# A feed-forward branch spread over 46 instead of 41 gaps, and half of an elementwise product moved from VectorE to GpSimd

## The reference, cut to what matters

```python
h = concat([class_token, patches @ W + b]) + pos_emb; h = concat([h, txt])        # [32, 274, 192]
# mixer: two selective scans, forward and backward, over layernorm(h)
def _selective_scan(dt, Bm, Cm, u, A, Dp):
    def step(h, inp):                       # state [384, 16] per image
        dA = exp(dt_t[..., None] * A)
        h = dA * h + (dt_t * u_t)[..., None] * B_t[:, None, :]
        y = einsum('bdn,bn->bd', h, C_t)
...
h = h + layernorm(x + (x_fwd + x_bwd))      # ends in "residual" and "add_mixer"
# feed-forward branch: attention with 12 heads, then fc1, gelu, fc2
x = x + attention(layernorm(x));  x = x + mlp(layernorm(x))
```

## Time and profile before

| | |
|---|---|
| median of 3 runs | 6239.66 us (6232.26 to 6243.73) |
| the profiled execution's own time | 6226.78 us |
| its span in the profile | 6225.0 us |
| DVE busy | 4946.1 us (79%) |
| PE busy | 4535.1 us (73%), mean granted clock 0.781 |
| ACT busy | 3184.2 us (51%) |
| POOL busy | 1.5 us |

### The profile page before, as it was taken

One profiled execution on the slowest core, in us unless ns is written; L12 is line 12 of the kernel. 1 busy time (PEld: TensorE's weight loads), 2 busy tenths in 40 slices (PEclk: granted clock), 3 DMA queues, 4 the chain that ended last, 5 costly groups with the idle time before them and its releaser, 6 DMA issues.

```text
span 6225.0 us, 69654 instructions
## 1 busy us (share of the span) xinstructions
PE 4535.1 (73%) x23852; PEld 2538.8 (41%) x23852; DVE 4946.1 (79%) x3712; ACT 3184.2 (51%) x6914; POOL 1.5 (0%) x9
## 2 busy tenths in 40 slices
PE   4677777777777777777777777777777777777777
PEld 2344434444343444434344443444344444444433
DVE  4988888888888888888887778877787878778771
ACT  2555555555455455555555555555554545555542
POOL 0000000000000000000000000000000000000000
PEclk7788877878777787777788877787787877788775
DMA  5877767767766776776686666666656666666740
GB/s 133 198 181 176 163 157 168 165 148 166 173 156 157 169 171 141 177 165 154 158 184 150 142 161 155 148 146 150 158 134 154 144 159 156 141 153 143 164 108 2
DMA packets 182837, 953.78 MB, mean 153 GB/s; under 512 B 26557, under 2 KB 76157, under 8 KB 84042
## 3 DMA queue, kind: packets, MB, share of 16 engines
q1 hardware_dynamic: 182442, 948.83, 66.2%
HBM read 888.14 MB, written 60.60 MB: 152 GB/s over the span
## 4 chain that ended last, share of the span: by engine, by line
PE 40%; DVE 31%; issue 17%; ACT 9%; DMA 2%; DVEq 1%; SPq 0%; ACTq 0%; POOL 0%; POOLq 0%
DVE hs L1077 9%; DVE hs L1066 6%; DVE neg_max L1171 5%; PE f_ps L636 5%; PE f_ps L682 4%; DVE hs L1083 3%; PE f_ps L551 3%; PE y_ps L475 3%; PE f_ps L671 3%; PE f_ps L624 3%; PE a_ps L511 3%; PE f_ps L560 3%; PE a_ps L521 2%; PE f_ps L576 2%; PE f_ps L593 2%
## 5 line engine op out<-in xcount | busy, mean ns | idle before, releaser
L1077 DVE TENSOR_TENSOR_SCAN hs<-decay,hs 128x2192 f32<-128x2192 f32 x384 | 1810.5, 4715 | 0.1
L831 ACT ACTIVATE decay<-decay,a_cols 128x273 f32<-128x273 f32 x3072 | 1377.8, 511 | 0.4
L1066 DVE TENSOR_TENSOR hs<-hs,b_ps 128x2192 f32<-128x2192 f32 x384 | 929.6, 2421 | 17.5 <-DMA hs<-dtu_rows 17.5
L1083 DVE TENSOR_TENSOR hs<-hs,c_s 128x2192 f32<-128x2192 f32 x384 | 933.6, 2431 | 7.7 <-issue 7.7
L511 PE MATMUL a_ps<-xn,w_in_s 96*128 96x274 f32 x1536 | 535.0, 478 | 244.8 <-ACT xi L854 171.6
L1171 DVE TENSOR_REDUCE neg_max<-f_ps 92x4 f32<-92x1096 f32 x288 | 371.6, 1290 | 355.3 <-PE f_ps L616 355.3
L923 ACT ACTIVATE hid<-f_ps 92x1096 f32<-92x1096 f32 x288 | 311.2, 1081 | 667.0 <-PE f_ps L624 666.6
L475 PE MATMUL y_ps<-hs,y_pick 128*32 128x274 f32 x6144 | 546.7, 483 | 33.3 <-DVE hs L1083 33.3
L511 PEld LDWEIGHTS a_ps<-xn,w_in_s 96*128 96x128 f32 x1536 | 326.2, 226 | 435.8 <-ACT xi L854 225.7
L624 PE MATMUL f_ps<-hid 32*92 32x274 f32 x1536 | 185.8, 562 | 379.5 <-ACT hid L923 202.6
L576 PE MATMUL f_ps<-cen,w_qk_s 96*128 96x274 f32 x768 | 284.2, 512 | 146.0 <-DVE cen L1109 111.2
(11 more groups left out here) (147 smaller groups left out, 6049.0 us busy)
## 6 DMA issues: line engine op xcount, KB each, us to landing
decay<-dt_rows SPq DMA_DIRECT2D x384, 1096.0 KB, 8.5
hs<-dtu_rows SPq DMA_DIRECT2D x384, 1096.0 KB, 12.4
dt_rows<-dt SPq DMA_DIRECT2D x192, 137.0 KB, 9.2
dtu_rows<-dtu SPq DMA_DIRECT2D x192, 137.0 KB, 9.4
xp<-in_patches SPq DMA_DIRECT2D x32, 588.0 KB, 16.7
out<-h SPq DMA_DIRECT2D x32, 205.5 KB, 10.9
h<-in_txt SPq DMA_DIRECT2D x32, 57.8 KB, 2.9
w_in_s<-in_w_in SPq DMA_DIRECT2D x1, 1152.0 KB
```

The costliest lines, as they stand in the source:

```text
L831: e = act.activation(dec[:, k, t], dec[:, k, t], ACT.Exp, scale=a_cols[:, d * IC + u, TILES * half + k:TILES * half + k + 1])
L1066: dve.tensor_tensor(x[:, :, :], x[:, :, :], b_ps[:, 0:T].unsqueeze(1).broadcast_to([128, TILES, T]), ALU.mult).then_inc(dbu_done, 1)
L1077: dve.tensor_tensor_scan(i, a, i, 0.0, ALU.mult, ALU.add).then_inc(scan_done, 1)
L1083: dve.tensor_tensor(x[:, :, :], x[:, :, :], c_s[d][:, :].unsqueeze(1).broadcast_to([128, TILES, T]), ALU.mult).then_inc(hc_done, 1)
```

## The change

1. The branch is stretched: the image e now ends at gap 45 instead of 40 (`LAST`). Centring, variance and scaling get a gap each (`SCALE_GAPS` is new); the score slots begin at gap 12 instead of 10; the division by the sums stands at gaps 24, 30, 33 instead of 21, 27, 29; fc1 moves from gaps 34, 35 to 38, 39, and so into gaps 2 and 3 of the next step; fc2 from 37, 38 to 41, 42.
2. Consumers move a gap behind their producers: a new `fine_first` at the head of a gap holds DVE's row maxima and divisions, and ACT's exponentials and copies, for what PE made in the gap before. On PE, `av`, all `spread_sums` and `proj` move from `fine_early` to `fine_late`.
3. Banks are dealt out anew (`CENTRE_BANKS`, `AV_BANKS`, `SUM_BANKS`, `VARIANTS`), `sq_f` gets a tile of its own, and `residual` writes `cen` instead of `res`, so that it needn't wait for the end of image e. The bias of the mixer's norm is added to `h` there, ahead of the scaled part.
4. The output projection of the mixer (`out_proj`) moves from gaps 32, 33 and 39 to gaps 35 (units 0 to 2), 37 (3 and 4) and 39 (unit 5). SP's store of the output stands behind `read_half(b, 5)` instead of `read_half(b, 4)`.
5. `output_product` on DVE covers tiles 0 to 3; a new GpSimd program multiplies tiles 4 to 7, on a semaphore of its own (`hc_pool`), for which `sum_states` and `c_copy` wait too.

```diff
-        CENTRE_GAPS = (5, 7, 32)
-        VAR_GAPS = (6, 8, 33)
...
+        CENTRE_GAPS = (5, 8, 35)
+        VAR_GAPS = (6, 9, 36)
+        SCALE_GAPS = (7, 10, 37)
...
+            def output_product(b, q):
+                d, x = q // 6, hs[q % 4][:, POOL_TILE:TILES, :]
+                pool.wait_ge(c_copied, at(b, 2, d + 1))
+                pool.wait_ge(scan_done, at(b, SCANS, q + 1))
+                pool.tensor_tensor(x, x, c_s[d][:, :].unsqueeze(1).broadcast_to([128, TILES - POOL_TILE, T]),
+                                   ALU.mult).then_inc(hc_pool, 1)
...
             def sum_states(b, q):
                 wait(pe, hc_done, at(b, SCANS, q + 1))
+                wait(pe, hc_pool, at(b, SCANS, q + 1))
...
                 dve.wait_ge(c_copied, at(b, 2, d + 1))
-                dve.tensor_tensor(x[:, :, :], x[:, :, :], c_s[d][:, :].unsqueeze(1).broadcast_to([128, TILES, T]),
+                x = x[:, 0:POOL_TILE, :]
+                dve.tensor_tensor(x, x, c_s[d][:, :].unsqueeze(1).broadcast_to([128, POOL_TILE, T]),
                                   ALU.mult).then_inc(hc_done, 1)
...
             def residual(f):
                 dve.wait_ge(out_mm, at(f, 1, 1))
-                wait(dve, out_ready, at(f, 1, 0))
-                dve.tensor_tensor(res[:, :, :], f_ps[0:CH, 3:5, 0:T], xn[parity(f)][:, :, :], ALU.add)\
+                dve.tensor_tensor(cen[:, :, :], f_ps[0:CH, 3:5, 0:T], xn[parity(f)][:, :, :], ALU.add)\
                     .then_inc(r_ready, 1)
...
+            def fine_first(f, gap):
+                if 0 <= gap - 1 - SLOT_GAP < len(SLOTS):
+                    kind, g, t = SLOTS[gap - 1 - SLOT_GAP]
+                    if kind == "s":
+                        row_maxima(f, g, t)
+                if gap in NORM_GAPS:
+                    divide_sums(f, NORM_GAPS.index(gap))
```

More of the change, by code:

```diff
@@ L344, in endings @@
         def endings(d, gap, f, e):
-            if d == 0 and gap <= 4 and e is not None:
+            if d == 0 and gap <= LAST and e is not None:
                 yield (*e, 2 * GAPS + gap)
@@ L428, in step @@
                 read_half(b, 5)
+                if e is not None:
+                    store(e[0])
                 write_rows(b, 1, 0)
@@ L456, in _, with step @@
             pool.memset(v_mask[0:1, 1:3], 0.0).then_inc(s_cp, 1)
+            def output_product(b, q):
[4 more added lines that the diff above has]
+                                   ALU.mult).then_inc(hc_pool, 1)
+            def step(b, f, e, a):
+                for q in range(SCANS):
+                    output_product(b, q)
+            program(step, pool.Fori, lambda: None, lambda f, e: None)
         @block.tensor
@@ L705, in fine_early @@
                     v_mms(f, 1)
[L706 to L711, removed]
             def fine_late(f, small, gap):
@@ L715, in fine_late @@
                     v_mms(f, 0)
+                if gap in AV_GAPS:
+                    av(f, AV_GAPS.index(gap))
                 if 0 <= gap - SLOT_GAP < len(SLOTS):
@@ L727, in fine_late @@
                     q_with_maxima(f, MAX_GAPS.index(gap))
-                if gap == SUM_GAPS[2]:
-                    spread_sums(f, 2)
+                if gap in SUM_GAPS:
+                    spread_sums(f, SUM_GAPS.index(gap))
+                if gap == PROJ_GAP:
+                    proj(f, small)
                 if gap in FC1_GAPS:
                     fc1_mms(f, small, FC1_GAPS.index(gap))
[L732 to L737, removed]
+                if gap in FC2_GAPS:
+                    fc2_mms(f, small, 0, (FC2_GAPS.index(gap),))
+                if gap == FC2_GAPS[1] + 2 and small:
+                    fc2_mms(f, small, 2, (0,))
+                if gap == 1:
+                    out_proj(f, (3, 4))
+                if gap == 3:
+                    out_proj(f, (UNITS - 1,))
             def fronts(b, d, a, gap):
@@ L805, in finish @@
             def finish(f, e):
-                for gap in range(2 * GAPS + 5):
-                    if gap <= 4:
+                for gap in range(2 * GAPS + LAST + 1):
+                    if gap <= LAST:
                         fine_early(*e, 2 * GAPS + gap)
@@ L1016, in step @@
                     for gap in range(GAPS):
+                        for ending in endings(d, gap, f, e):
+                            fine_first(ending[0], ending[2])
                         q = d * 6 + gap // 3 + 1
@@ L1048, in finish @@
             def finish(f, e):
-                for gap in range(2 * GAPS + 5):
-                    if gap <= 4:
+                for gap in range(2 * GAPS + LAST + 1):
+                    if gap <= LAST:
+                        fine_first(e[0], 2 * GAPS + gap)
                         fine_mid(*e, 2 * GAPS + gap)
                         fine_late(*e, 2 * GAPS + gap)
+                    fine_first(f[0], gap)
                     fine_mid(*f, gap)
```

147 lines of the change are left out of this document (74 added, 73 removed).

## The result

The changed kernel takes 5836.45 us (median of 3, 5832.26 to 5839.99) against 6239.66 us. The ratio is 0.9355, 95% interval 0.9334 to 0.9376. The forecast was 5540 us.

The account below looks back on a forecast made before the run. DVE, fullest at 79%, was taken as held by waits of 1092.4 us. Large steps going from 181 to 160 us and small from 197 to 172 summed to 695 us saved, hence 5540 us; range 5230 to 5950.

Parts of the forecast that it names:

- the allowance for waits: Time added per step for handing over between in-order lists: 1.3 us in the first ten gaps, 2.3 in the other 26.
- the first part: A step's first ten gaps, as the prediction counted them: forecast 60 us in a large step, 70 in a small one.
- the worth of DVE's time: Per step, DVE was to get back 13.6 us from halved output products and pay 9.6 us beside GpSimd.
- The halved product: DVE's output product on 1096 instead of 2192 elements: 1.30 us, saving 1.13 us, 12 times a step.
- POOL's product: GpSimd's multiplication of its half of the output product: 2.5 us taken, with 1.0 and 5.0 us kept as limits.
- the rivals of 3.5 and 4.4 us: GpSimd's half takes longer: 5910 us at 3.5, whole gain spent at 4.4; chances 0.13 still faster, 0.11 slower.
- POOL beside DVE: Cost to DVE's short two-SBUF-input instructions while GpSimd works after a scan: 9.6 us a step, range 0 to 30.
- The rival "free": GpSimd working beside DVE costs DVE nothing, instead of 9.6 us a step: 5290 us; chance 0.25.
- the rule: Trainium skill's shared-port rule: GpSimd would also hold DVE's scalar-operand instructions after q 0, 1 and 3, estimated 5 us a step.
- Waits moved: Sign to look for: DVE's waits at row maxima, divisions and scalings go from over 800 to under 150 us.
- the rival by which spacing only moves the waits: PE falls behind in the first ten gaps; half of DVE's 1092 us of waits stays: near 6000 us; chance 0.06.
- PE as the bound of the first part: In the first ten gaps PE has 58.7 us of work (large step) or 70.3 (small), more than DVE.

Follow-up runs that it names:

- e1: The changed kernel without its GpSimd program, DVE multiplying all eight tiles (the stretched branch alone): 5722.6 us, ratio 0.9175.
- e10: e1 with 20 and 14 extra throwaway matmuls a step on TensorE, where it stood idle for row maxima: 5610.8 us, ratio 0.9003.
- e9: e1 with the output product left out for tiles 4 to 7, which no engine multiplies: 5592.5 us, ratio 0.8984.
- e3: e1 with three GpSimd products on constants after each scan, results used by nobody: 5972.5 us, ratio 0.9576.
- e12: The changed kernel with 20 and 14 extra throwaway matmuls a step on TensorE: 5793.8 us, ratio 0.9286.
- e13: e12 with eight more matmuls in the second place (20 and 22): 5663.6 us, ratio 0.9075.
- e11: e9 with 20 and 14 extra throwaway matmuls a step on TensorE: 5443.4 us, ratio 0.8719.
- e5: The changed kernel with the second division by the sums one gap later (gap 31 instead of 30): 5859.5 us, ratio 0.9391.
- e7: The changed kernel with DVE's input product directly behind the scan in ten of twelve half-units, so that it covers GpSimd: 6002.1 us, ratio 0.9628.
- e6: The changed kernel with GpSimd taking its half only after four scans (q 5, 6, 9, 11), DVE multiplying all tiles otherwise: 5744.0 us, ratio 0.9233.

## Why the forecast was right in direction and 296 us off in size

**The first step that failed is the allowance for waits: "For handing over between in-order lists I add 1.3 us in the first part and 2.3 in the second".** It had no row behind it. The prediction's own sum without the GpSimd half gives 5552 us: the first part stays at PE's 60 and 70 us, and in the second DVE would have 98.1 and 102.3 in place of 97.7 and 101.9, so 0.4 us a step, 12 us in 31. e1 is that kernel and took 5722.6, so 170 of the 296 us were missed in the stretched branch. In its second part DVE stands idle 8.6 us in a large step (105.8 us, 97.2 busy) and 9.5 in a small one (108.3, 98.8 busy), not 2.3. At the division a further scan, an input product and five short instructions (the prediction counts four) do stand in between, but PE's work before it ran at half clock; with PE kept busy (e10) the wait there is 26.6 us, and e10 lies 59 us above the 5552. That the clock would be low just behind PE's waits was nowhere in the prediction, though the earlier trace rows show mean clocks of 0.75 to 0.81. A slip is in it too: the small steps, 70 + 102, got next to nothing of the allowance; with it they are 71.6 + 104.2, some 50 us more over 13 steps.

**The second is the worth of DVE's time: "So DVE gets back 13.6 and pays 9.6".** In the sum this was a gain of 12 us; e1 and the changed kernel show a loss of 114, the other 126 of the 296 us. Both lengths were nearly right, what they are worth was not. Work taken from the output product was worth 0.30 of its length (e9), and 286 of the 427 us came back as idle time of DVE. The 353 us of stalls cost 244 us, or 0.69, and those of e3 250 for 303, or 0.82. The stalls fall on instructions for whose results, directly or in DVE's list behind them, PE and ACT stand idle. That this makes their price is shown for the part that goes through the clock (e12 against e13); the rest of it is argued. Nor is it separated that PE also waits for POOL's half.

**The halved product**: forecast 1.30 us, measured 1289 ns. **POOL's product**: forecast 2.5 us, measured 2348 ns; the rivals of 3.5 and 4.4 us fall.

**POOL beside DVE**: forecast 9.6 us a step, measured 353 / 31 = 11.4. The instructions with two SBUF tensors make 8.3 of that (258.8 / 31); the scalar-operand ones, which I had left to the rule at an estimated 5, make 3.0. The rival "free" (5290 us) falls; e11 took 5443 us with POOL's half costing nothing at all and the clock held.

**Waits moved**: the row maxima, divisions and scalings were to go from over 800 to under 150 us; they went from 813 to 421. So this sign failed, and the rival by which spacing only moves the waits was partly right (94.2 us at `dt` and 90.2 at `cen`); but half of the waits went. e5 shows that one of them, the division's, can't be removed by its own place.

**PE as the bound of the first part** came out right in its number and by luck. From a step's first scan to that of q 4 a large step takes 61.6 us (forecast 60), the rest 108 (forecast 100); a small one 73.2 (70) and 110.6 (102). But PE isn't full there. The two parts of a large and of a small step of the changed kernel, and the first part of each in the kernel before (columns as in the earlier trace rows):

```profile
1756.30:1818.60 62.30, 53.96 (x258) 34.63 (x256) 55.23 (x50) 37.99 (x84) 9.28 (x4) 0.87 0.77 179
1818.60:1929.70 111.10, 76.36 (x475) 38.57 (x474) 96.20 (x64) 55.54 (x124) 18.94 (x8) 0.78 0.79 179
4206.80:4274.80 68.00, 59.56 (x294) 39.82 (x292) 55.28 (x53) 46.56 (x99) 9.26 (x4) 0.95 0.64 151
4274.80:4389.20 114.40, 81.33 (x480) 40.37 (x480) 97.76 (x68) 55.39 (x123) 18.93 (x8) 0.76 0.81 183
```

```profile
1863.80:1925.70 61.90, 48.55 (x260) 30.77 (x260) 56.22 (x48) 36.19 (x80) 0.00 (x0) 0.89 0.64 145
4498.90:4574.40 75.50, 58.84 (x294) 37.29 (x293) 57.76 (x51) 42.95 (x91) 0.00 (x0) 0.87 0.50 112
```

PE has as many matmuls there as before (258 and 260, 294 and 294) and over eleven large steps is busy 52.8 us (51.3 before), not 58.7, so it stands idle for 8.8 us of the 61.6. The prediction added fc1 and two units of the output projection and took nothing away: I named the windows of the earlier trace rows wrongly, they hold twelve and 24 gaps, not ten and 26, and the first score blocks and part of the queries, which stood in those twelve gaps, left them when the score slots moved from gap 10 to 12. The rest of the time goes into waits of the engines for each other, again the allowance that was too small.

What stays open: the 53 us that remain between e13 and e10 were not taken apart, nor the waits at the first row maximum (2.9 to 3.5 us a large step in e10) and at fc2.

## What to carry to other kernels

Price an offload by who waits for what is freed and for what is slowed, not by busy time: here 427 us freed from the output product were worth 0.30 of their length (0.39 with PE kept busy, 0.40 in the order of e7, nothing for the 132 us of e6), and 353 us of stalls on short instructions that others wait for cost 0.69. Before moving elementwise work to GpSimd, list what VectorE does in the two to three microseconds after its start; where that is short work on SBUF tensors that another engine waits for, leave it. When TensorE waits several microseconds in every step, compare the same matmul ahead of and behind the wait: if it takes 1.7 to 1.9 times as long behind, putting throwaway matmuls into the wait can be worth more than the offload (112 and 173 us here).

## What the hardware showed that I had not expected

- TensorE's granted clock had a large share in what a late VectorE instruction cost here. Eight more throwaway matmuls a step (22 in place of 14), some 2.6 us of extra work, took 130 us off the program.
- A scalar-operand instruction with one SBUF tensor is held by GpSimd as one with two is: the two on `cen` take up to 2.23 us from the start of the first to the end of the second beside POOL, and 0.75 without.
- The hold goes both ways. Beside short instructions nearly all of the loss is DVE's: POOL's product took 2320 ns where mostly the input product stood beside it (e7), and 2348 where it met short ones. Where DVE does its output product and scan, POOL is the one held, up to 9.7 us for a product of 1.0 (e3).
- Behind each second step of a loop DVE stands 4.8 to 6.2 us at the first output product with no engine to wait for ("issue", 58.4 us in 11 waits; 7.7 us in 8 before). It is in all stretched kernels, e1 and e10 too (58.0 and 57.9 us). PE stands some 4 us near the same place, but did so before as well (60.4 us in 11 waits). The cause is open.
